# An attention block on one core: the order of VectorE's, ScalarE's and GpSimd's work, and of the end

## The reference

```
x = input (2, 512, 512);  xn = layernorm(x)
q, k, v = xn @ Wq.T, xn @ Wk.T, xn @ Wv.T     # 32 query heads, 8 key/value heads, 128 wide
q, k = rmsnorm(q) * wq, rmsnorm(k) * wk
attn = softmax(q k.T / sqrt(128) - slope * distance, causal)     # ALiBi
s = (attn v) @ Wo.T
g = silu(low-rank mixture of 8 experts of rank 16 on xn)
y = x + s * g
```

## Time and profile before

| | us |
|---|---|
| median of 3 runs | 757.17 (757.09 to 758.48) |
| the profiled execution, its own time | 757.56 |
| its span, first to last instruction | 755.4 |
| PE busy / DVE / ACT / POOL | 720.2 / 596.5 / 562.5 / 363.9 |

### The profile page before, as it was taken

The page is one execution under the profiler, slowest core; times in us unless marked ns, Lnnn a source line. Parts: engine busy times, 40 slices in busy tenths (PEclk is TensorE's granted clock), DMA queues, the critical chain, the costliest instruction groups (busy, mean ns, idle before and its releaser), DMA issues.

```text
span 755.4 us, 14576 instructions
## 1 busy us (share of the span) xinstructions
PE 720.2 (95%) x3736; PEld 609.3 (81%) x3736; DVE 596.5 (79%) x1468; ACT 562.5 (74%) x1440; POOL 363.9 (48%) x343
## 2 busy tenths in 40 slices
PE   7998999999999999999999999999999999999795
PEld 7787888878888788888888788888888788887665
DVE  6858798778977798678987789687987789777774
ACT  4567787788777788686877887777876877878672
POOL 4225354446444653464534653644544554436256
PEclk9999999999999999999999999999999999999999
DMA  8015969678786868687695777768686786867632
GB/s 298 1 29 151 291 165 260 172 209 231 193 257 159 236 177 243 194 233 222 165 282 146 218 219 216 228 174 258 162 251 173 216 237 181 262 158 194 196 130 83
DMA packets 215877, 148.68 MB, mean 197 GB/s; under 512 B 49072, under 2 KB 206640, under 8 KB 215728
## 3 DMA queue, kind: packets, MB, share of 16 engines
q1 hardware_dynamic: 180720, 128.43, 58.4%
q10 hardware_dynamic: 35136, 20.00, 10.6%
HBM read 86.17 MB, written 62.19 MB: 196 GB/s over the span
## 4 chain that ended last, share of the span: by engine, by line
PE 44%; issue 16%; DVE 13%; ACT 9%; POOL 7%; DMA 4%; SPq 3%; ACTq 2%; DVEq 0%; POOLq 0%
PE qkv_ps L1271 4%; PE qkv_ps L1272 4%; PE qkv_ps L1273 4%; PE out_ps L1271 4%; PE out_ps L1273 4%; PE out_ps L1272 4%; DMA qk_moved<-turning_qk 3%; ACT probs L672 3%; SPq L444 3%; PE score_ps L1271 3%; PE score_ps L1273 2%; PE mix_ps L1271 2%; PE score_ps L1272 2%; PE mix_ps L1273 2%; PE mix_ps L1272 2%
## 5 line engine op out<-in xcount | busy, mean ns | idle before, releaser
L546 POOL TENSOR_TENSOR pt_lo<-x_sb,pt_hi 128x512 fp32r<-128x512 f32 x137 | 174.5, 1298 | 263.3 <-ACT pt_hi L734 263.3
L664 ACT ACTIVATE probs<-probs,neg_max 128x128 f32<-128x128 f32 (+3 forms) x256 | 142.0, 559 | 47.2 <-DVE neg_max L954 46.5
L954 DVE CUSTOM_DVE_ANT_0 probs<-score_ps,cst,slope 128x128 f32<-128x128 f32 (+3 forms) x256 | 129.5, 546 | 33.8 <-PE score_ps L1273 25.2
L672 ACT ACTIVATE probs<-probs,recip 128x128 f32<-128x128 f32 (+3 forms) x252 | 126.3, 549 | 8.2 <-DVE recip L961 8.2
L1271 PE MATMUL qkv_ps<-w_hi,xt_hi 128*128 128x256 f32 (+1 forms) x392 | 126.4, 322 | 2.4 <-DVE xt_lo L897 1.4
L1272 PE MATMUL qkv_ps<-w_lo,xt_hi 128*128 128x256 f32 (+1 forms) x392 | 126.4, 322 | 0.0
L1273 PE MATMUL qkv_ps<-w_hi,xt_lo 128*128 128x256 f32 (+1 forms) x392 | 126.0, 321 | 0.0
L1271 PE MATMUL out_ps<-wo_hi,o_hi 128*128 128x512 f32 x252 | 101.6, 403 | 3.3 <-DVE o_lo L998 3.3
L536 POOL TENSOR_TENSOR inv_rms<-sums,minus_half 128x5 f32<-128x5 f32 x64 | 78.6, 1228 | 52.9 <-DVE sums L1012 52.8
L975 DVE STREAM_TRANSPOSE squared<-probs 128x256 f32<-128x256 f32 (+3 forms) x124 | 101.8, 823 | 1.2 <-ACT probs L672 0.3
L1273 PE MATMUL out_ps<-wo_hi,o_lo 128*128 128x512 f32 x252 | 99.8, 396 | 0.0
(11 more groups left out here) (172 smaller groups left out, 1626.1 us busy)
## 6 DMA issues: line engine op xcount, KB each, us to landing
turning_qk<-qk_squared ACTq DMA_DIRECT2D x244, 80.0 KB, 2.0
qk_moved<-turning_qk SPq DMA_DIRECT2D x61, 320.0 KB, 3.4
turning<-squared SPq DMA_DIRECT2D x120, 128.0 KB, 2.4
x_sb<-turning SPq DMA_DIRECT2D x30, 512.0 KB, 5.1
w_raw<-wqkv SPq DMA_DIRECT2D x32, 384.0 KB, 5.2
turning<-squared SPq DMA_DIRECT2D x120, 96.0 KB, 2.0
x_sb<-turning SPq DMA_DIRECT2D x30, 384.0 KB, 4.2
turning<-squared SPq DMA_DIRECT2D x128, 64.0 KB, 1.8
```

The lines of the kernel that those rows point to most:

```text
L546: nc.gpsimd.tensor_tensor(by_quad(pt_lo, j), moved_block(t, j), by_quad(pt_hi, j).bitcast(F32), ALU.subtract).then_inc(pt_lo_by_pool, 1)
L664: nc.scalar.activation(probs[:, h, 0:n], probs[:, h, 0:n], ACT.Exp, bias=neg_max[:, h:h + 1], scale=-1.0, accum_out=total[:, h:h + 1]).the ...
L672: nc.scalar.activation(to[:, h, 0:n], probs[:, h, 0:n], ACT.Copy, scale=recip[:, h:h + 1]).then_inc(probs_ready, 1)
L954: nc.vector.tensor_tensor_reduce(probs[:, h, 0:n], score_bank(t, h), cst[:, C_DIST + SEQ - n:C_DIST + SEQ], slope[:, h:h + 1], HUGE, ALU.a ...
```

## The change

The diff, cut to its core; further lines only carry the counts of the new semaphores (`w_lo_by_dve`, `w_lo_by_pool`, `wo_lo_by_pool`, `wo_lo_by_dve`, `x_again`) to their waits.

- In wide units VectorE's `mixed_lo(t-3)` comes after `bias(t, 0)`, in the slot after the one in which it was; before a narrow unit `mixed_lo(t-2)` comes before `square_probs(t, 2)`.
- ScalarE does `mixed_hi` before `write_qk`, but for slot 2.
- One of the four `wo_lo` goes from GpSimd to VectorE (end of slot 2), and a third `w_lo` of four (slot 5).
- GpSimd's `turned_lo(t-1)` waits for q_lo and k_lo of unit t+1.
- In the last group q and k of unit 7 are turned by five transposes on TensorE (`turn_last_qk`), kept in the buffers of the weights; SyncE reads those of unit 6 before the second pair of unit 4 is written; GpSimd does the inverse of unit 7 before `turned_lo(3)`, and `finish_y` of blocks 0 and 1 in slots 4 and 5; the order of `end` is new on all engines.
- In the prologue VectorE makes `wo_lo` of head 2.

```diff
+WO_POOL, WO_DVE = (0, 1, 3), 2
 BY_TURN = QB - 1
 EARLY_W = 2
+W_DVE = 3
...
+        last_q = w_hi[:, 0, 0:QW], w_lo[:, 0, 0:QW]
...
-        gate_tanh = [wo_raw[:, 2 + m % 2, :] for m in range(BLOCKS)]
+        gate_tanh = [wo_raw[:, (m + 2) % 4, :] for m in range(BLOCKS - 2)]
+        gate_tanh += [part[:, :, :].rearrange("p a n -> p (a n)")[:, 0:DM] for part in (qk_squared, qk_moved)]
...
+        def last_turned_ps():
+            return turned_ps()[0], qkv_ps[:, 0, 0:P].rearrange("p (a n) -> p a n", a=QUADS)
...
+        def by_squares(t, left):
+            return here(t, left) and not is_last(t, left)
+        def is_last(t, left):
+            return left == 1 and t == BLOCKS - 1
...
+            def move(g, t, u, soon=False):
                 i, to = t % QB, moved[t % 2]
                 n = (i + 1) * P // 2
-                for pair in range(2):
-                    sp.wait_ge(probs_squared, TWO(g, t, pair + 1))
-                    for q in range(QUADS):
-                        sp.dma_start(turning[t % 2, q, :, pair * n:(pair + 1) * n].rearrange("(k r) n -> r k n", k=QUADS),
-                                     squared[q * QUAD:(q + 1) * QUAD, :, pair, 0:n]).then_inc(probs_written[pair], 16)
-                if u is not None:
-                    sp.wait_ge(qk_written, QK_WRITTEN(g, u - BY_TURN, 16 * QUADS))
-                    sp.dma_start(qk_moved[:, :, :], turning_qk[u % 2, :, :, :].rearrange("q p n -> p q n")).then_inc(qk_moved_ready, 16)
+                write_probs(g, t, 0)
+                if soon:
+                    sp.wait_ge(qk_lo_ready, K_AND_Q_LO(g, u, 0))
+                    read_qk(g, u)
...
+                write_probs(g, t, 1)
+                if u is not None and not soon:
+                    read_qk(g, u)
...
+                if left == 1 and t == 3:
+                    load_x_again(range(0, 2))
...
-                    move(g, t, t + 2 if here(t + 2, left) else None)
+                    move(g, t, t + 2 if by_squares(t + 2, left) else None, left == 1 and t == W_SLOT - 1)
...
-                if left == 1:
-                    load_x_again(range(2 * (t - 3), 2 * (t - 3) + 2))
...
-                    load_x_again(range(BLOCKS - 2, BLOCKS))
+                    load_x_again(range(2, BLOCKS))
...
-                pool.wait_ge(w_lo_by_dve, group * EARLY_W)
+                pool.wait_ge(w_lo_by_dve, group * W_DVE)
...
-                if t % BLOCKS == W_SLOT:
+                if t % BLOCKS == W_SLOT and here(t + 3, left):
                     turned_lo(g, t - 2)
                 if here(t + 2, left):
                     inverse_rms(g, t + 2)
                 if t % BLOCKS == W_SLOT and here(t + 3, left):
-                    split_w(g + 1, range(EARLY_W, KC))
+                    split_w(g + 1, range(W_DVE, KC))
+                elif t % BLOCKS == W_SLOT:
+                    turned_lo(g, t - 2)
                 if t % BLOCKS == 2 and here(t, left) and t > 2:
-                    split_wo(g + t // BLOCKS, range(0, HPG))
+                    split_wo(g + t // BLOCKS, WO_POOL)
+                if left == 1 and t == 4:
+                    finish_y(0)
                 if here(t - 1, left) and not by_both(t - 1):
+                    pool.wait_ge(qk_lo_ready, K_AND_Q_LO(g, t + 2, 0))
+                    if left == 1 and t == W_SLOT:
+                        finish_y(1)
                     turned_lo(g, t - 1)
...
                 turned_lo(g, BY_PE - 1)
-                pool.wait_ge(x_again, 16 * BLOCKS)
-                for m in range(4):
+                for m in range(2, BLOCKS - 2):
                     finish_y(m)
                 start_last_y()
-                for m in range(4, BLOCKS - 2):
-                    finish_y(m)
...
+                    elif m in (4, 5):
+                        act.wait_ge(gate_done, m - 3)
+                    elif m == 6:
+                        act.wait_ge(qk_written, QK_WRITTEN(GROUPS - 1, BLOCKS - 1 - BY_TURN, 0))
+                    elif m == 7:
+                        act.wait_ge(qk_lo_ready, K_AND_Q_LO(GROUPS - 1, BLOCKS - 1, 0))
...
-                if left == 1 and t < W_SLOT:
-                    gate_tangents(range(2 * (t - 3), 2 * (t - 3) + 2))
+                if left == 1 and t == 3:
+                    gate_tangents(range(0, 2))
+                if left == 1 and t == 4:
+                    gate_tangents(range(2, 6))
...
-                if here(t + 2, left):
+                if wo_due:
                     write_qk(g, t + 2)
-                if wo_due:
                     act.wait_ge(out_ready, ONE(g, t - 2, 0))
                     split_wo(g + t // BLOCKS, range(0, HPG))
                 if here(t - 2, left):
                     mixed_hi(g, t - 2, left)
+                if by_squares(t + 2, left) and not wo_due:
+                    write_qk(g, t + 2)
...
-                exponentials(g, before, range(0, HPG))
-                turned_qk_hi(g, last)
+                turned_qk_hi(g, last, True)
+                exponentials(g, before, range(0, 3))
                 for pair in range(2):
                     act.wait_ge(probs_written[pair], WRITTEN(g, before, 0))
                 normalize_probs(g, before, range(0, 2), late_probs)
                 mixed_hi(g, before - 2, 1)
+                exponentials(g, before, range(3, HPG))
                 normalize_probs(g, before, range(2, HPG), late_probs)
                 moved_hi(g, before - 1)
-                gate_tangents(range(4, 6))
-                exponentials(g, last, range(0, 3))
+                gate_tangents(range(6, BLOCKS))
+                exponentials(g, last, range(0, 2))
                 mixed_hi(g, before - 1, 1)
                 for n in range(keys_of(before)):
                     turned_hi(before, n)
-                exponentials(g, last, range(3, HPG))
+                exponentials(g, last, range(2, HPG))
...
+            def split_wo(group):
+                dve.wait_ge(wo_hi_done, group * HPG + (WO_DVE + 1))
+                nc.vector.tensor_tensor(wo_lo[:, WO_DVE, :], wo_raw[:, WO_DVE, :], wo_hi[:, WO_DVE, :].bitcast(F32),
+                                        ALU.subtract).then_inc(wo_lo_by_dve, 1)
...
+            def w_slot(g, t):
                 square_sums(g, t + 2)
                 value_lo(g, t + 2)
                 for h in range(HPG):
                     bias(g, t, h)
                 moved_lo(g, t - 2)
-                if w_due:
-                    split_w(g + 1, range(0, EARLY_W))
-                else:
-                    turned_qk_lo(g, t + 1)
+                split_w(g + 1, range(0, W_DVE - 1))
+                normalize_k(g, t + 2)
+                reciprocals(g, t, 0)
+                reciprocals(g, t, 2)
+                split_w(g + 1, range(W_DVE - 1, W_DVE))
+                normalize_q(g, t + 2)
+                square_both(g, t + 2)
+                add_out(g, t - 3)
+                square_probs(g, t, 0)
+                turned_qk_lo(g, t + 1)
+                square_probs(g, t, 2)
+                set_factor(g, t + 3)
+            def last_w_slot(g, t):
+                square_sums(g, t + 2)
+                value_lo(g, t + 2)
+                for h in range(HPG):
+                    bias(g, t, h)
+                moved_lo(g, t - 2)
+                reciprocals(g, t, 0)
+                reciprocals(g, t, 2)
+                turned_qk_lo(g, t + 1)
                 normalize_k(g, t + 2)
                 normalize_q(g, t + 2)
-                reciprocals(g, t, 0)
-                square_both(g, t + 2)
-                reciprocals(g, t, 2)
                 add_out(g, t - 3)
                 square_probs(g, t, 0)
-                if w_due:
-                    turned_qk_lo(g, t + 1)
+                mixed_lo(g, t - 2, 1)
                 square_probs(g, t, 2)
-                mixed_lo(g, t - 2, left)
-                if w_due:
-                    set_factor(g, t + 3)
+            def wide(t):
+                return keys_of(t) >= 3
             def slot(g, t, left):
+                if t % BLOCKS == W_SLOT and left == 1:
+                    last_w_slot(g, t)
+                    return
                 if t % BLOCKS == W_SLOT:
-                    w_slot(g, t, left)
+                    w_slot(g, t)
                     return
                 if here(t, left):
                     bias(g, t, 0)
+                if here(t - 3, left) and wide(t):
+                    mixed_lo(g, t - 3, left)
...
+                if here(t - 2, left) and not wide(t + 1):
+                    mixed_lo(g, t - 2, left)
                 if here(t, left):
                     square_probs(g, t, 2)
-                if here(t - 2, left):
-                    mixed_lo(g, t - 2, left)
-                if left == 1 and t == 4:
-                    multiply_gate(range(2, 4))
...
+                if t % BLOCKS == 2 and here(t, left) and t > 2:
+                    split_wo(g + t // BLOCKS)
...
-                for h in range(HPG):
-                    bias(g, before, h)
```

(31 more changed lines are left out.)

98 lines of the change are left out of this document (58 added, 40 removed).

## The result

The changed kernel took 749.5 us (median of four runs, 746.84 to 750.34) beside 757.13 us for the kernel before: ratio 0.9877, 95% interval 0.9843 to 0.9912. (The ratio on record is not quite the quotient of the two medians, which is 0.9899; where the two differ I give both.) Timed once more (experiment 9) it took 746.5 us beside 757.63, ratio 0.9854. By the medians the gain is 7.6 us in the first and 11.1 in the second, by the ratios 9.3 and 11.1, against 11.4 forecast.

A forecast was written before the change was run, and what follows sets the result against it. TensorE, busy 95% of the span, was taken as the bound, with its waits in the bodies and the end to win. First body 1.3, six bodies 2.4, end 7.7: 11.4 us, giving 745.8 us; range 737 to 753.5.

The forecast's parts named there:

- rival C: End gives half, as VectorE's list becomes its bound: 3.9 us less, 750 us; chance 0.15.
- The end, forecast 7.7: Last stretch, 64.30 us long before: fewer TensorE waits and a shorter tail save 7.7 us.
- (a): End, wait of 1.16 us before unit 6's scores: SyncE reads q and k earlier, 0.3 us saved.
- (b): End, wait of 3.62 us: bias(6, 0) starts earlier, saving 3.6 and 1.2 of clock; new waits 0.5 and 0.4.
- (c): End, wait of 1.69 us for q_hi(7): read from PSUM, all saved (1.7); five transposes cost 0.7.
- (d): Tail: four finish_y pieces move to slots 4 and 5, GpSimd is done before VectorE: 2.5 us saved.
- The bodies, forecast 3.7: Loop bodies: 1.3 us saved in the first, 2.4 in the other six, 0.4 in each.
- So k_lo of unit 6 is not later: Slot 5: third w_lo costs VectorE 0.9 us, paid by a shorter q_lo; slot 6 begins 0.3 to 0.4 earlier.
- I give back 0.3: Slot 4: TensorE is 0.65 us early, but mix(3) needs low parts by DMA that come no earlier; 0.3 lost.
- the weights give 0.5: First body: the weights were to save 0.5 us of its 1.3.
- P: Slot 2: GpSimd takes the port, VectorE's wo_lo waits 1.26 us more, TensorE sees it in six bodies: 753 us; chance 0.09.
- D: Wide slots: o_lo behind bias(t, 0) comes too late for out(t-3), kernel slower, 761 us at 0.5 average; chance 0.08.

The follow-up runs named there:

- experiment 9: The changed kernel timed again with no edit: 746.5 us beside 757.63 us for the kernel before, ratio 0.9854.
- experiment 1: The changed kernel with the edits of the bodies undone, all but the dropped wait for k_lo of units 0 and 4: 749.3 us, ratio 0.987.
- experiment 10: The kernel of experiment 4 with GpSimd's old tail, finish_y of blocks 0 and 1 back in the end: 748.6 us.
- experiment 4: The changed kernel with VectorE's gate products of blocks 4 to 7 put behind o_lo in the end: 745.9 us, ratio 0.9833.
- experiment 2: The kernel before with the edits of the bodies alone and its old end: ratio 0.9977, 1.7 us faster.
- experiment 5: The kernel of experiment 4 with mixed_lo back at the end of each slot in the bodies: 760.6 us.

## Why the prediction was right, and where it was not

The sum came out, and in part by luck: the end gave more than forecast, the start 1.9 us in the profile where 0.4 was forecast, and the bodies gave less. 749.5 is also the number of rival C (750), but not by C's account, in which the end gives half.

**The end, forecast 7.7, measured 8.9 and 8.4** in the two profiles (64.3 to 55.4 and 55.9) and 9 to 10 in time by experiment 1. (a) and (b) came as worked out: unit 6's scores wait for nothing and begin 18.7 us after the mark for 19.1 (0.4, 0.3 forecast), bias(6) no longer holds TensorE, the clock stays full, and GpSimd and VectorE take turns before `mix(3)` (0.66 idle). The new wait before scores(7) is 0.43 of excess for 0.4 forecast; the one of `out(3)` for o_lo, 0.5 forecast, did not come, and (b) gave more than 3.6 for it. (c) held: nothing waits for unit 7's q. (d) held (experiment 10), and is the only term of the end that was tried singly; (a) to (c) rest on the rows. Rival C's sign, a new wait above 1 us between 716 and 735, did show: 1.81 us, by its mechanism. Taking that wait out did not shorten the end (56.0, experiment 4), so it did not cost the 3.9 us of C.

**The bodies, forecast 3.7, measured 1.7 alone; on top of the new end between 0.5 lost and 1.2 won** (0.9877 and 0.9854 against 0.9870). In slots 2 to 5 the body was read nearly rightly. Neg_max has 0.16 to 0.2 of excess left, o_lo 0.17, there is one `w_lo` wait in six of the seven bodies, and q_lo takes 0.65 in slot 5. One of these was not the forecast's: k_lo's wait in slot 4 is gone because `scores` no longer waits there, not because k_lo came earlier (experiment 2 still has that wait, at 0.6). Counted from unit 2's scores, the mean of the later bodies (kernel before, then the two profiles of the changed one) shows where the gain went:

| us from the start of unit 2's scores | before | changed | again |
|---|---|---|---|
| TensorE begins unit 4's scores | 22.2 | 21.5 | 21.6 |
| SyncE issues the second read of unit 3's probabilities | 27.6 | 27.4 | 27.5 |
| it lands | 33.1 | 33.7 | 33.0 |
| GpSimd's last `w_lo` ends | 43.7 | 43.3 | 42.9 |
| k_lo of unit 6 ends | 44.5 | 44.8 | 44.4 |
| TensorE begins unit 6's scores | 44.9 | 44.9 | 44.5 |

TensorE is 0.7 us earlier at unit 4, but the read of unit 3's probabilities is not, and the high parts, low parts, `w_lo` and k_lo stand behind its landing. So 0 to 0.4 us of the 0.7 are left at unit 6, the forecast's "0.3 to 0.4" in the better profile. From there to the next unit 2 another 0.2 to 0.3 are lost, in a stretch that the forecast took to be without a break: in some bodies k_lo before unit 2's scores (0.4 of excess) or a low part before a mix (0.45), where the kernel before has no wait. Against a forecast of 86.4 a body and 0.4 won, the later six bodies are 87.0 us before and 87.2 and 86.9 after. The sum failed in three steps.
- "So k_lo of unit 6 is not later": it is not, but TensorE is, by the waits removed, earlier. So it waits 0.4 us of excess there in every body, which I had not priced. (The third `w_lo` and what moved with it start q_lo 0.8 to 1.2 us later, and q_lo is 0.87 shorter.) I checked what was late against the old clock of TensorE, not the new.
- "I give back 0.3" before `mix(3)`: 0 to 2.05 us, by when one read of 512 KB lands. It took 5.6 to 7.5 us from its issue in the later six bodies of the first profile and 5.0 to 5.9 in those of the second. In the first one body pays 2.05 and two others 0.8; that and the first body are most of its 3 us over the second.
- First body, "the weights give 0.5": they cost. The "0.4 of small operations" ahead of the third `w_lo` are reciprocals that wait for ScalarE's exponentials, 0.42 and 0.82 us in the first body, and TensorE waits 0.75 and 0.85 for weights where it waited 0.46. That is the first profile; the second has 0.85 before one of them. The first body took 88.0 and 87.2 us after 86.4. The wait before unit 3's scores, for which 0.4 was forecast, went from 1.45 to 1.25 and 1.38.

**P and D.** The port went right in the changed kernel (`wo_lo` 0.85 us on VectorE, between the bounds of 0.65 and 1.53) and went wrong as soon as `mixed_lo` stood ahead of it (1.73 us, experiment 5). By the Trainium skill (SBUF — State Buffer, Who interferes with whom) the ports that VectorE and GpSimd share are an exclusive lock, and the order of issue decides who waits; the long pieces of 1.53 and 1.73 agree with it, 0.65 alone and less than the GpSimd piece beside them (1.83 and 1.27) on top. I gave the two moves, of `mixed_lo` and of `wo_lo`, some 0.3 us a body between them; undone singly they cost 14.7 and 7.4 us. Undone together with the rest they cost nothing (experiment 1). D did not happen: no wide slot of the changed kernel has an excess over 0.2 us before `out`.

## What to carry to other kernels

A wait that is removed makes the waiting engine early for all that follows: check each later meeting of the engines against the new time, or the gain is spent at the next one; here twelve of fourteen profiles, with quite different waits, have 86.4 to 87.2 us as the mean of their six later bodies. In this loop the meeting that held was a transfer that did not start earlier when TensorE did. Edits of an order written by hand are not a sum: undo each singly before it is called useful or useless, since of the five here two cost nothing undone, the others 5 to 8, 7 and 15 us, and all undone together cost about 1 at most. The end of the program, where nothing comes after to absorb a shift, paid 8 to 10 us. There work taken off the path (GpSimd's products, earlier) gave what the rows said when it was undone; the transfer replaced by five transposes was judged from the rows alone, where unit 7's q is no longer waited for.

## What the runs showed that I had not expected

- Whether a wait costs the clock too is not decided by its length alone. The same wait of 1.81 us before `out(5)` in the changed kernel, then in the kernel of experiment 1, and that of 1.98 us in another body of experiment 5; windows behind each:

```profile
728.40:732.00 3.60, 3.59 (x15) 2.92 (x16) 2.37 (x6) 2.94 (x6) 3.44 (x4) 1.00 0.30 113
```
```profile
728.90:732.20 3.30, 3.30 (x10) 2.57 (x9) 0.83 (x3) 1.33 (x2) 2.74 (x3) 0.51 0.23 84
```
```profile
338.50:342.70 4.20, 4.12 (x18) 3.37 (x19) 3.85 (x14) 3.60 (x10) 3.05 (x4) 1.00 1.05 348
```

  The clock stayed at 2.4 GHz in the first, fell to 1.2 in the second, and stayed in the third. Where it fell it cost 1.5 us in a body (89.2 for 87.7), and in the end some 1.8: behind the wait nine matmuls begin 0.15 to 0.20 us late each. (The end of experiment 1 is 1.9 us longer than the changed kernel's, but it also has a wait of 0.91 for o_lo that the other lacks.) What decides it was not tried.
- The order in which two instructions of VectorE and GpSimd arrive sets the price: the same VectorE subtraction among GpSimd's `wo_lo` took 0.85 us in seven bodies of seven, and 1.72 to 1.74 in seven of seven one position later in the list, where (in the body shown) it starts 0.09 us behind the start of a GpSimd piece of 1.27 us.
- In the profile's columns small waits count as busy matmul time: a body with 85.7 us "busy" and one with 85.3 did the same work in 86.6 and 86.9 us.
